# Adding bfloat16 filler matmuls on the identity to TensorE's program in the context MLP and routing stage

## What is computed

```python
    def _L1_xattn_ref(x, w1, w2):
        h = jnp.einsum('eth,efh->etf', x, w1)
        g = jax.nn.gelu(h, approximate=True)
        out = jnp.einsum('etf,efh->eth', g, w2)
        return out
    ...
    x = x + _L1_xattn_ref(_layernorm(x, axis=-1), ctx_1024, ctx_1024)
    x = x + _L1_ffn_ref(_layernorm(x, axis=-1), L1_ffn_w_router, L1_ffn_w1, L1_ffn_b1, L1_ffn_w2, L1_ffn_b2)
```

## Time and profile before

| | |
|---|---|
| median of 3 runs | 744.81 us (739.28 to 745.09) |
| the profiled execution, its own time | 744.16 us |
| its span, first to last instruction | 742.4 us |
| mean granted TensorE clock over the span | 0.895 |

### The profile page before, as it was taken

One profiled execution on the slowest core, in us unless ns is written; L12 is line 12 of the kernel. 1 busy time (PEld: TensorE's weight loads), 2 busy tenths in 40 slices (PEclk: granted clock), 3 DMA queues, 4 the chain that ended last, 5 costly groups with the idle time before them and its releaser, 6 DMA issues. The chain is left out here.

```text
span 742.4 us, 12123 instructions
## 1 busy us (share of the span) xinstructions
PE 599.1 (81%) x3667; PEld 521.3 (70%) x3668; DVE 498.7 (67%) x950; ACT 292.4 (39%) x536; POOL 321.5 (43%) x271
## 2 busy tenths in 40 slices
PE   4588999953579999999999985675668959687984
PEld 4467888953468888888888872465557847576874
DVE  4698888855027888889889864774376636536562
ACT  1144554512146878778788701332012102111210
POOL 3344434421413344344344311250166956697265
PEclk9799999995699999999999997955579989988997
DMA  6111111100344232322322005323032451422110
GB/s 211 29 45 42 30 28 29 29 9 0 90 112 86 47 81 44 83 47 57 72 45 43 0 1 193 134 87 149 20 121 73 156 182 36 174 101 84 43 28 18
DMA packets 24823, 53.10 MB, mean 72 GB/s; under 512 B 4570, under 2 KB 11483, under 8 KB 22730
## 3 DMA queue, kind: packets, MB, share of 16 engines
q1 hardware_dynamic: 20474, 45.10, 20.6%
q0 software_dynamic: 2208, 5.41, 2.6%
q10 hardware_dynamic: 2096, 2.05, 0.9%
HBM read 31.55 MB, written 4.87 MB: 49 GB/s over the span
## 5 line engine op out<-in xcount | busy, mean ns | idle before, releaser
L881 POOL TENSOR_SCALAR h_p<-h_p,h_rs 128x1024 f32<-128x1024 f32 x64 | 72.5, 1132 | 131.5 <-DVE h_rs L973 131.5
L980 DVE TENSOR_REDUCE h_nmx<-h_psS 128x1 f32<-128x1024 f32 x64 | 78.1, 1221 | 22.4 <-PE h_psS L1071 21.0
L960 DVE TENSOR_TENSOR h_pTl<-h_psT,h_pTh 128x512 fp32r<-128x512 f32 x128 | 81.5, 678 | 4.4 <-ACT h_pTh L908 4.4
L908 ACT CAST h_pTh<-h_psT 128x512 fp32r<-128x512 f32 x128 | 69.2, 590 | 29.6 <-PE h_psT L1031 29.6
L930 ACT ACTIVATE h_p<-h_psS,h_nmx 128x1024 f32<-128x1024 f32 x64 | 72.3, 1129 | 17.7 <-DVE h_nmx L980 17.7
L1042 PE MATMUL h_psO<-h_pTh,h_vs 128*128 128x256 f32 x256 | 70.0, 307 | 3.1 <-DVE h_oT L968 2.3
L308 POOL TENSOR_TENSOR a_p<-a_p,a_rs 128x616 f32<-128x616 f32 x32 | 39.0, 1220 | 73.9 <-DVE a_rs L355 73.9
L1031 PE MATMUL h_psT<-ident,h_p 128*128 128x128 f32 x512 | 67.4, 273 | 1.4 <-DVE h_pTl L960 1.2
L1031 PEld LDWEIGHTS h_psT<-ident,h_p 128*128 128x128 f32 x512 | 59.1, 141 | 11.2 <-issue 3.3
L1042 PE MATMUL h_psO<-h_pTl,h_vs 128*128 128x256 f32 x256 | 63.8, 282 | 0.0
L1504 POOL TENSOR_TENSOR wl<-wst,wh 128x1024 fp32r<-128x1024 f32 (+1 forms) x18 | 56.0, 3114 | 2.7
(11 more groups left out here) (262 smaller groups left out, 1506.3 us busy)
## 6 DMA issues: line engine op xcount, KB each, us to landing
wst<-in_m_w SPq DMA_DIRECT2D x16, 1024.0 KB, 5.9
bias<-in_m_b SPq DMA_DIRECT2D x8, 640.0 KB, 8.6
h_kh<-h_hi SPq DMA_DIRECT2D x32, 128.0 KB, 2.4
h_kl<-h_lo SPq DMA_DIRECT2D x32, 128.0 KB, 2.4
rows<-x_all SPq DMA_DIRECT2D x4, 516.0 KB, 3.4
a_qs<-a_qhi SPq DMA_DIRECT2D x16, 128.0 KB, 2.3
a_qs<-a_qlo SPq DMA_DIRECT2D x16, 128.0 KB, 2.3
h_qs<-h_hi SPq DMA_DIRECT2D x16, 128.0 KB, 2.2
```

Source lines behind the costliest of these rows:

```text
L881: pool.tensor_scalar(pr[:, u % 4], pr[:, u % 4], rs[:, u:u + 1], 0.0, ALU.mult, ALU.add).then_inc(pn_ready, 1)
L908: act.copy(pTh[u // QP % 2][:, hf * HK:(hf + 1) * HK, u % QP * P:(u % QP + 1) * P], psT[hf][:]).then_inc(pT_hi, 1)
L960: vec.tensor_tensor(pTl[u // QP % 2][part], psT[hf][:], pTh[u // QP % 2][part], ALU.subtract).then_inc(pT_lo, 1)
L980: vec.tensor_reduce(nmx[:, u:u + 1], psS[u % 2][:], AX.X, ALU.max, negate=True).then_inc(max_ready, 1)
```

## The change

PE's stream gets a helper that issues n matmuls into columns 0 to 255 of `psC`, a bank that nothing reads until the counting matmuls have written it anew. The weights are the first 128 of the 256 bfloat16 columns that the float32 identity makes when its bits are taken as bfloat16, the moving operand is all 256. These matmuls wait for no semaphore and raise none. There are 24 at the stage's start, 8 in each `hidden`, 4 in `output(0)` and 10 in each other `output`, 8 in each `route`, 10 before each of the two last transposes, and 40 after the last `route`. All in all they are 24 + 4 x 8 + 4 + 3 x 10 + 4 x 8 + 2 x 10 + 40 = 182.

```diff
         def _(pe):
+            units = ident[:].bitcast(BF16)
+
+            def keep_busy(n):
+                for _ in range(n):
+                    pe.matmul(psC[:, 0:256], units[:, 0:P], units, start=True, stop=True)
+
+            keep_busy(24)
             pe.wait_ge(t["c_in"], 48)
...
             def hidden(n):
+                keep_busy(8)
                 pe.wait_ge(xT_sb, n + 1)
...
             def output(n):
+                keep_busy(10 if n else 4)
                 pe.wait_ge(g_ready, n + 1)
...
             def route(n):
+                keep_busy(8)
                 pe.wait_ge(xT_sb, NC + n + 1)
...
             for n in range(1, NC):
                 if n + 1 < NC:
+                    keep_busy(10)
                     transpose(NC + n + 1)
                 route(n)
+            keep_busy(40)
             pe.wait_ge(consts, 1)
             pe.wait_ge(oh_ready, 1)
```

## The result

The kernel with the fillers takes 749.16 us (median of 16 runs, 746.42 to 752.15), the one before 743.74 (16 runs, 739.28 to 745.45). The ratio is 1.0075, with a 95% interval of 1.0058 to 1.0093: by the ratio 5.6 us slower (the medians are 5.4 apart), where 7.0 were forecast. The profiled execution takes 749.70 us, its span is 747.3, the mean granted clock 0.915 (0.895 before). So the clock is better and the kernel is slower.

What follows compares the result with a forecast made beforehand. DVE and POOL were taken to bound the stage's middle, PE its tail, half its work at 1.2 GHz. Terms: -0.15 - 0.65 + 3.4 + 4.8 - 0.4 = +7.0 us on 744.16, 751.2 us; range 742.8 to 757.5.

Steps and rivals of the forecast that it cites:

- The price of a filler: One filler matmul on PE: 0.118 us at full clock and 0.213 at half clock, taken from rows of 256-column matmuls.
- Part 1: Stage's start, 24 fillers, first hiddens and output(0): T(0) later but work behind at full clock; -0.15 us (-0.6 to +0.9).
- Part 2: Loop while the clock is up: fillers fit PE's waits, the clock doesn't fall at 481, T(4) gets faster; -0.65 us.
- Part 3: Gap before the last transpose: PE's idle time widens from 2.4 to 5.1 us, so the clock is low there.
- Part 4: Tail from the last transpose: route groups of 8 cost +3.4 us, the 40 +4.8, faster counts -0.4, inversion stays 7.04.
- The step that was mis-sized: 40 fillers after the last route: 6.6 us with the clock rising 4.2 us in, less 1.77 hidden wait, +4.8 us.
- the two lags: Dense PE streams at the low clock: 3.3 to 5.1 us until the clock rises; middle 4.2 taken.
- C: Fillers on the identity, start to tail, don't lift the clock: +14.8 us, 759.0 us; chance 0.12.
- A: Tail: last transpose and the 8 fillers behind it lift the clock once more; +3.7 us, 747.9 us; chance 0.18.
- B: Clock held right through, from the idle time before the last transpose into the tail; -0.6 us, 743.6 us; chance 0.15.
- My theory: A filler costs its duration where PE is on the path, nothing where PE waits; the clock gives back little.

Runs made afterwards that it cites:

- experiment 5: The change with 46 fillers instead of 10 before the last transpose, tail fillers kept; ratio 0.9987 to the kernel before, stage 79.38 us.
- experiment 1: The change without its 40 fillers after the last route; ratio 1.0030 to the kernel before, stage 83.06 us.
- experiment 7: The change with 46 fillers before the last transpose and none behind it; ratio 0.9946 to the kernel before, stage 75.75 us.
- experiment 2: The change without the 8 fillers in each of route(2) and route(3), the 40 kept; ratio 1.0040 to the kernel before, stage 83.28 us.
- experiment 4: The change without the 24 fillers at the stage's start; ratio 1.0086 to the kernel before, stage 86.14 us.
- experiment 6: experiment 3 plus 34 fillers into psX in PE's wait between counts and inversion; ratio 0.9928 to the kernel before, stage 76.47 us.
- experiment 8: The change without tail fillers, with 46 before the last transpose and 34 before the inversion; ratio 0.9907 to the kernel before, rerun 734.60 us and 0.9898.
- experiment 3: The change without any filler behind the last transpose (route(2), route(3), the 40); ratio 0.9994 to the kernel before, stage 79.77 us.
- experiment 11: experiment 8 plus 8 fillers in the wait for the one-hot; 735.80 us, ratio 0.9922 to the kernel before.
- experiment 9: experiment 7 plus 48 unread route-form calls (96 rows on PE) at the end of route(3); ran once, no timed ratio given.

## Why the prediction was right, and where it was off

Direction and place were right, and the size was within the range: +5.6 measured, +7.0 forecast.

- *The price of a filler.* 0.213 at the low clock is what the two groups of 8 show (1.71 and 1.66). At the full clock the 40 take 4.37 us in experiment 5 (503.32 to 507.69), 0.109 each, not 0.118. The rows that I took were of another kind of matmul. The estimate of 109 ns, worked out from the Trainium skill (page "TensorE: Matmul & The Clock Gate", section "Back-to-back issue gap"), was the right one.
- *Part 1* (-0.15 forecast): -0.52. T(0) came 4.05 us after the stage's start, where 455.55 had meant 4.67, because the clock rose 3.0 us behind the first filler and not 4.2. In the twelve profiles with the 24 it came after 4.0 to 4.3 us.
- *Part 2* (-0.65): -0.67 from O(0) to T(7), with T(4) at 1.04. The loop's fillers fitted their gaps, with 0.23 and 0.73 us to spare. They are no guarantee, though. In the profile of experiment 1, whose loop is the same, the clock was down from 486.7 to 493.6, with O(3) at 3.75 us, and next to nothing was lost by it: T(7) started 49.8 us into the stage (451.76 to 501.56), against 49.6. That is the claim that DVE and POOL set the pace there, seen from the other side.
- *Part 3*: an idle time of 4.97 us before T(7) (5.1 forecast) and the clock at 0.50 behind it. That the widening of the wait is the reason is not shown, though. In the profile of experiment 1 the wait was 2.70 us, and the clock fell in it too, at 500.4, 1.5 us behind the last filler:

```profile
500.00:501.00 1.00, 0.00 (x0) 0.00 (x0) 1.00 (x2) 0.00 (x0) 0.71 (x1) 0.69 0.00 0
```

```profile
501.56 1.97 PE L1383 MATMUL c_psX<-ident,xg 128*128 128x128 f32 x8 [2.70 <-DVE xg L1271]
```

  What experiments 5 and 7 show is that the clock stays up when the wait is filled.
- *Part 4*: the two groups of 8 cost +3.22 (3.4 forecast). The counts gave -0.43 (-0.4), the inversion 7.04 as before.
- *The step that was mis-sized* is the 40 fillers: "together 6.6", less 1.77, so +4.8. They took 5.89 us, and the term was +3.97. The clock rose at 515.0, 3.2 us into them, below the shortest of the two lags that I had bracketed (3.3 to 5.1 us). Two rows were too few for a bracket. The lag is no constant even of one kind of stream: the 40 have 3.2 us here and in experiment 2 and 3.7 in experiment 4, the 34 before the inversion 3.5 to 4.2. The trace of the kernel before had two longer ones besides, which I passed over: the experts' matmuls that start at 533.30 were lifted at 539.1, and those that start at 550.90 at 556.2. My estimate with 0.109 at the full clock and the rise 4.2 us in is 6.4 for the 40: so about 0.5 of the 0.7 us between 6.6 and 5.89 came from the rise and 0.2 from the price. Why the rise came at 3.2 us and not at 4.2 stays open.

**The rivals.** C, fillers that don't lift the clock, is out: they lifted it in every profile. A, a further lift by T(7) and its 8 fillers, happened in none of the three profiles with that order at the low clock (the change, experiments 1 and 4), which fits the rule of the Trainium skill that stood beside it (page "TensorE: Matmul & The Clock Gate", "Part 4: PE-mode transpose"). But 3.4 us of stream may simply have been too short here, since fillers alone ran for up to 4.3 us before the clock rose; no run tells the two apart. B, the clock held right through the tail, didn't happen in the kernel with the change. Experiment 5 makes it by filling the gap, and gives 0.9987 of the kernel before, where I had worked out -0.6 us (0.9992).

My theory named the terms rightly, but I drew the wrong conclusion from them: that there was little to be had in the tail from a better clock. Experiments 6 to 8 show 3.3 us in the inversion and 4.0 in T(7), R(2) and R(3), all on the path.

## What to carry to other kernels

A filler is free only where its engine waits, and it pays only where the work behind it is on the path and runs before the clock falls. So first find the waits that stand directly ahead of work on the path, fill those nearly to their end, and put nothing between a wait that has been filled and the work that it was filled for. Here 80 fillers in two such waits, of which experiment 3 had 10, took 7.3 us off the stage (79.8 to 72.4), while the change's 56 in the tail had added 6.6. The loop's fillers held the clock over a part where little of PE's work is on the path, and left it to fall in the wait ahead of the part where all of it is.

## What the runs showed of the hardware

- A clock that is up outlasts the last dense matmul by a time that differs from place to place. With PE idle it was 1.5 us (experiment 1), 2.7 (the change), 2.2 and 4.0 (the kernel before). With transposes, routes or the inversion behind the fillers it was 3.3 (experiment 11), 4.6 (experiment 9), 4.8 (experiment 6) and 5.8 us (experiment 7, 500.35 to 506.1). Whether that work puts the fall off wasn't separated, and the two groups overlap.
- The stream of routes, 8 columns behind full weight loads, shows PE busy for all or nearly all of the time, and in it the clock neither rose (503.4 to 510.2 before, 6.8 us at 0.50) nor stayed up (experiment 9, then 20 us at 0.50).
- Such streams follow the clock: 32 rows in 3.64 us at 1.00 and in 6.83 at 0.50, the inversion's 32 with 50 columns in 3.75 and in 7.04.
- The clock rose under fillers whose weights and data are nearly all zeros. In ten of the twelve profiles with the 24 it rose 2.9 to 3.3 us behind the first of them, in the other two 4.2 to 4.3.
- In these two (experiments 1 and 9) the clock was still up when the 24 began, and fell under them, 0.8 us in, though they ran without a gap: at 452.6 with the first at 451.75, up again at 456.0 in experiment 1. A busy stream doesn't at once undo the idle time before it.
